# Token stages: the second product and all that follows it one pipeline step later, at the head of each engine's order

## The reference

```python
    x = x + _L0_conv_ref(_ln_c(x), ...)
    t = _to_tokens(x)
    t = t + _L0_ffn_ref(_ln_t(t), W1, b1, W2, b2)
    x = _from_tokens(t, x)
    x = x + _L1_conv_ref(_ln_c(x), ...)
    t = _to_tokens(x)
    t = t + _L1_ffn_ref(_ln_t(t), W1, b1, W2, b2)
...
        h = jax.nn.relu(_qlinear(x, W1, b1))
        y = _qlinear(h, W2, b2)
```

## Time and profile before

| | us |
|---|---|
| median of three runs | 2622.84 |
| lowest, highest | 2618.95, 2629.99 |
| the profiled execution, its own time | 2624.89 |
| its span | 2623.1 |
| TensorE, busy time in the span | 2272.7 (87%) |
| VectorE, ScalarE, GpSimd, busy | 1523.5, 1123.3, 450.0 |

### The profile page before, as it was taken

The page is one execution under the profiler, slowest core; times in us unless marked ns, Lnnn a source line. Parts: engine busy times, 40 slices in busy tenths (PEclk is TensorE's granted clock), DMA queues, the critical chain, the costliest instruction groups (busy, mean ns, idle before and its releaser), DMA issues. The chain is left out here.

```text
span 2623.1 us, 62156 instructions
## 1 busy us (share of the span) xinstructions
PE 2272.7 (87%) x21290; PEld 1247.5 (48%) x21290; DVE 1523.5 (58%) x2653; ACT 1123.3 (43%) x2338; POOL 450.0 (17%) x707
## 2 busy tenths in 40 slices
PE   6679778898996999999699999999976998688886
PEld 3344436667773333333266666666641232233332
DVE  3345401111113777777488888888842455577776
ACT  4346421111112888888532222222211111577776
POOL 7510015100100000000054444444410000000000
PEclk9789869999997999999899999999987999899999
DMA  6999989788874777877576666666628999333332
GB/s 154 260 254 270 253 284 303 230 263 262 285 245 91 142 142 146 152 142 145 100 155 144 142 142 142 142 143 143 144 86 162 240 267 237 87 102 106 105 102 78
DMA packets 533239, 458.55 MB, mean 175 GB/s; under 512 B 316476, under 2 KB 445444, under 8 KB 529778
## 3 DMA queue, kind: packets, MB, share of 16 engines
q1 hardware_dynamic: 462882, 425.87, 63.4%
q0 software_dynamic: 5744, 23.34, 3.7%
q10 hardware_dynamic: 64512, 7.88, 2.3%
HBM read 272.33 MB, written 186.40 MB: 175 GB/s over the span
## 5 line engine op out<-in xcount | busy, mean ns | idle before, releaser
L604 PE MATMUL gate_ps<-gate_data,gate_wt 64*64 64x289 f32 x6144 | 397.1, 416 | 39.2 <-issue 27.2
L604 PEld LDWEIGHTS gate_ps<-gate_data,gate_wt 64*64 64x64 f32 x6144 | 303.1, 136 | 134.3 <-issue 59.8
L662 DVE TENSOR_TENSOR gate_out<-gate_gelu,gate_ps 128x578 f32<-128x578 f32 x96 | 72.2, 756 | 399.3 <-PE gate_ps L604 343.7
L949 ACT CAST mix_h<-mix_bank 96x512 f16<-96x512 f32 x512 | 267.6, 593 | 7.1 <-PE mix_bank L900 3.2
L639 ACT ACTIVATE gate_gelu<-gate_ps 128x578 f32<-128x578 f32 x96 | 62.7, 653 | 367.8 <-PE gate_ps L604 331.2
L2036 PE MATMUL fus_bank<-fus_xt,fus_taps 76*32 76x512 f32 x1344 | 159.6, 626 | 28.4 <-DMA fus_shift<-gate_shift 23.5
L1031 DVE TENSOR_SCALAR mix_hb<-mix_h,mix_b1q 96x1024 f16<-96x1024 f16 x256 | 122.7, 479 | 93.6 <-ACT mix_h L949 93.6
L900 PE MATMUL mix_bank<-mix_xq,mix_w1q 112*96 112x512 fp8e5 x512 | 143.5, 382 | 29.1 <-ACT mix_h L949 23.0
L1039 DVE CAST mix_hq<-mix_hb 96x2048 fp8e5<-96x2048 f16 x128 | 156.5, 1223 | 19.5 <-DVE mix_hb L1031 16.9
L292 DVE COPY exp_out<-exp_y 128x384 f32<-128x384 f32 x192 | 102.1, 567 | 103.5 <-PE exp_y L255 52.1
L912 PE MATMUL mix_x_bank<-mix_hq,mix_w2q 96*112 96x512 fp8e5 x512 | 136.1, 388 | 29.9 <-DVE mix_hq L1039 27.7
(11 more groups left out here) (226 smaller groups left out, 4050.6 us busy)
## 6 DMA issues: line engine op xcount, KB each, us to landing
y<-exp_out SPq DMA_DIRECT2D x64, 816.0 KB, 12.2
gate_data<-y SPq DMA_DIRECT2D x24, 2176.0 KB, 17.6
g<-gate_out SPq DMA_DIRECT2D x48, 578.0 KB, 4.9
mix_sc<-g SPq DMA_DIRECT2D x31, 816.0 KB
gate_wt<-wm SPq DMA_DIRECT2D x96, 256.0 KB, 8.5
wav_strips<-xp SPq DMA_DIRECT2D x96, 204.0 KB, 3.8
wav_halves<-xp SPq DMA_DIRECT2D x48, 340.0 KB
init<-wav_init SPq DMA_DIRECT2D x48, 268.0 KB, 2.4
```

What stands on the lines that cost most here:

```text
L604: mm = pe.matmul(banks(a, v)[64 * g:64 * (g + 1), r], wt[q][64 * r:64 * (r + 1), 2 * a + g, n, :], src, start=n == 0, stop=n == 3)
L949: act.copy(h16[at.pair][:, m, h, :], bank[(2 * m + h) % len(bank)][0:HID, :]).then_inc(h16_ready, 1)
```

## The change

In both stages, `show`, `round_shown` and `add_shown` move from stage 3 to stage 4 and to the head of the lists of PE, ACT and DVE. What follows them (`centre_out`, `variance("out")`, `square("out")`, `root("out")`, `normalise`, both stores) also goes one stage later, in its old place of the list. On DVE `add_shown` now stands ahead of `add_residual`, on PE `show` stands ahead of `project`. `quantize_hidden` gets a wait: `hq` has two buffers, and the second product of step n-2 must be done with the one that step n writes. `LEAD` of the second stage goes from 4 to 8. No instruction that computes is added or removed.

```diff
-        LEAD = 12 if wide else 4
+        LEAD = 12 if wide else 8
...
-                staged(sp, 2 * N, SLOTS, [(0, load), (4, store_x2)] + [(7, store_norm)] * wide, LEAD)
+                staged(sp, 2 * N, SLOTS, [(0, load), (5, store_x2)] + [(8, store_norm)] * wide, LEAD)
...
-                pieces = [(0, project), (3, show), (2, hide(0)), (2, hide(1)), (1, variance("in")), (0, centre_in)]
+                pieces = [(4, show), (0, project), (2, hide(0)), (2, hide(1)), (1, variance("in")), (0, centre_in)]
                 if norm_dst is not None:
-                    pieces = [(0, project), (3, show), (2, hide(0)), (4, centre_out), (2, hide(1)), (1, variance("in")), (5, variance("out")), (0, centre_in)]
+                    pieces = [(4, show), (0, project), (2, hide(0)), (5, centre_out), (2, hide(1)), (1, variance("in")), (6, variance("out")), (0, centre_in)]
...
-                pieces = [(3, round_shown), (2, round_hidden(0)), (2, round_hidden(1)), (1, root("in")),
+                pieces = [(4, round_shown), (2, round_hidden(0)), (2, round_hidden(1)), (1, root("in")),
                           (0, square("in"))]
                 if norm_dst is not None:
-                    pieces = [(3, round_shown), (2, round_hidden(0)), (4, square("out")), (2, round_hidden(1)), (1, root("in")), (5, root("out")), (0, square("in"))]
+                    pieces = [(4, round_shown), (2, round_hidden(0)), (5, square("out")), (2, round_hidden(1)), (1, root("in")), (6, root("out")), (0, square("in"))]
...
                 def quantize_hidden(at):
                     dve.wait_ge(hb_ready, at.n + 1)
+                    if not isinstance(at.n, int) or at.n >= 2:
+                        dve.wait_ge(mixed, at.n - 1)
...
-                pieces = [(0, add_residual), (3, add_shown), (2, bias_hidden), (2, quantize_hidden), (1, quantize_norm)]
+                pieces = [(4, add_shown), (0, add_residual), (2, bias_hidden), (2, quantize_hidden), (1, quantize_norm)]
                 if norm_dst is not None:
-                    pieces.append((5, normalise))
+                    pieces.append((6, normalise))
```

## The result

The changed kernel takes 2649.78 us (median of 20 runs), the kernel before 2622.82 (median of 20). The ratio is 1.0091, with a 95% interval of 1.0065 to 1.0117: slower, by 27 us of the medians. The ratio leaves out two slow executions of the changed kernel (7396.48 and 2684.37 us); the median of the others is 2648.5. The forecast was 2634 with a range of 2605 to 2660.

The account below looks back on a forecast made before the run. The prediction took loops of waits to bound the stages, 6.94 us a step (first, PE) and 5.64 (second). +26 in the first, -12.6 in the second and -1.5 at its end give +11.7 on 2622.84: 2634 us, range 2605 to 2660.

Parts of the forecast that it names:

- the 5.64 loop: Second stage before the change: show, y16, hidden copies, hq and back to show, 5.64 us a step.
- The tie through x1's four slots: Both stages: x1 waits for the x2 just before it, a new one-step loop of 7.37 us (first), 5.43 (second).
- The wait for the logarithm at show: First stage: show at the head must wait for logarithm out, which project covered before; 0.25 us a step.
- Loop (b): First stage, PE and ACT alone: variance in to show, show, project, hide(0), hide(1); 7.25 us a step.
- the own wait: On DVE, x1 waits for the semaphore of the x2 just before it; taken as 0.04 us, at most 0.22.
- my own case: The forecast itself: 2634 us, own range 2615 to 2650, first stage at 7.2 to 7.5, second 5.3 to 5.5; chance 0.58.
- The -1.5 at the end of the second stage: Second stage's end: hide no longer stands behind a show waiting for hq; -1.5 us, between 0 and -3.
- The first (only the second stage feels it): Rival: first stage stays at PE's own 6.94 a step, the second gains; 2609 us, chance 0.12.
- The second (upper bounds of the two gaps): Rival: x2 to x1 and yb to x2 gaps on DVE both cost 0.22; 2667 us, chance 0.14.
- The third, that the own wait is free: Rival: DVE's waits on its own semaphore cost nothing, saving 0.33 in both tie loops; 2608 us, chance 0.07.
- The fourth: Rival: the change moves nothing, gains and losses fall on slack; 2623 us, chance 0.09.
- loop (a): First stage: show, y16, yb, x2, x1, variance in, both logarithms and back to show; 7.37 us a step.

Follow-up runs that it names:

- order-only kernel with a later store: Kernel before, second stage reordered at stage 3 (show behind hide, y16 behind hidden copies, add_shown last), x2 store one stage later, eight iterations written out: ratio 0.9897.
- The control: Kernel before with eight x1 buffers and loops unrolled by eight, nothing else changed: ratio 0.999, second stage at 5.64 a step.
- order-only run: Kernel before, second stage reordered at stage 3: show behind hide, y16 behind the hidden copies, add_shown last, four buffers, store unmoved: ratio 1.0175.

## Why the prediction was right, point by point

**The present loops.** The second stage's is confirmed: with the show taken out of its place the 5.64 loop disappears, and the order-only kernel with a later store cuts it another way. That PE holds the first stage at 6.94 was read from the rows and not tested; no kernel tried had a mean pitch below 6.96 there.

**The tie through x1's four slots.** This is shown, by both of its halves. Eight buffers take away the semaphore's part, the residual first takes away the order's part, and the second stage goes from 5.58 over 5.33 to 5.15. The control excludes the buffers as such.

**The wait for the logarithm at show.** This is shown too. Without the tie, putting project back ahead of show took the first stage from 7.33 to 6.98. The 0.25 read from the end of the first stage before is the 0.25 measured in its middle (1014.74 to 1014.99). Loop (b) is the next longest of the first stage: 7.25 forecast, 7.33 measured.

**The sizes.** The forecast had +0.43 a step in the first stage and -0.21 in the second; the pitches give +0.54 and -0.06. Two terms were too small, and both stand in both loops. `x2` to `x1` was taken as 0.73 and measured 0.79 to 0.83, 0.81 on average. The choice of 0.04 for the own wait, because "its other operands and counts are ready while the 0.69 run", was the step that failed; 0.10 to 0.14 is between my bounds, near the average gap of `yb` to `x2`, which was the nearer row. And variance to logarithm in the first stage, or variance to centre in the second, was taken from products that had not waited: 1.06 and 0.86, where behind a wait they are 1.15 and 0.94. The earlier trace rows had shown the longer record, 1.11, for a product behind a wait. Together these are 0.17 and 0.16 a step, where the pitches missed the sums of 7.37 and 5.43 by 0.14 and 0.15. That is some 8 to 9 us in each stage; the ends of the second stage (below) gave 2 us more than forecast, and in all the forecast was 15 us short.

**How right it was.** The direction, the two loops and the sign of each stage came out as forecast; the size did not. I had forecast 11 us more and measured 27. The two errors had the same sign, and the forecast was a difference of two larger terms, 26 and 14 us, so both counted in full. The 2650 us lie at the very edge of the range I gave for my own case (2615 to 2650), and both pitches lie just outside theirs (7.51 for 7.2 to 7.5, 5.58 for 5.3 to 5.5). That the time still lies inside the range of 2605 to 2660 owes something to its width. Of the three outcomes, "within 0.5%" had the highest chance (0.46); the one that came, slower by more, had 0.40.

**The ends.** The -1.5 at the end of the second stage was too small, and a cost at its beginning was taken as 0 and is not. The last three pitches are 3.41, 4.27 and 3.65, together 5.8 us less than the last three before, and the stage ends 0.9 sooner behind its last show; but the first show comes 3.1 later behind the first project (20.29 instead of 17.24). Together the ends gave 3.6 of the 7.2 us, and the pitch the rest.

**The rivals.** The first (only the second stage feels it) fell with the first stage's 7.51. The second (upper bounds of the two gaps) was half right: the `x2` to `x1` gap came out at 0.10 to 0.14 instead of 0.22, and the `yb` to `x2` gap at 0.21 to 0.24 in every other step of the first stage and 0.15 to 0.18 in the second, with 0.04 in the steps between. The third, that the own wait is free, is refuted by the run with eight buffers: the same two instructions are 0.61 apart without the wait and 0.80 to 0.83 with it. The Trainium skill, "VectorE: DVE Perf Modes", section "The DRAIN you can't avoid", speaks of a semaphore that is set after each copy. What costs here is the wait for it, and the page says nothing of that; that waits too are free was the prediction's own reading of it. No run here sets or leaves out a semaphore alone. The fourth fell with the 1.0091.

Costs taken as nothing: in the second stage the run with the first stage old shows none for stores, loads and the added wait. In the first stage, loop (a) with the measured terms (show to `y16` 1.08, `yb` 0.61, `x2` 0.48 on average, `x1` 0.81, its two parts 1.14, then 0.05, 1.15, 1.26, 0.67 and 0.25) is 7.50 against a pitch of 7.51, which leaves no room for them. That the loads keep their distance was right for this change, and the order-only run shows how it goes wrong when `x2` moves.

## What to carry to other kernels

Moving a piece to a later stage lengthens the life of what it reads: count the buffers, since the last free one turns a cross-iteration slack into a tie inside the iteration, and write the new one-step loop down before you gain from cutting the old one. Before a piece goes to the head of an engine's list, ask which wait the piece that stood there was covering. When a result moves on a compute engine, follow it to the DMA queue too, because the loads can stand behind its store.

## What the runs showed of the hardware that was not expected

The first product of PE behind a wait for `x1` takes longer to the next product than the same product without a wait: 0.94 or 0.95 (2414.09 to 2415.03, 2454.80 to 2455.75) against 0.86, with a recorded duration of 1.11 against 1.02. ACT, which waits for its result, starts 1.14 to 1.15 after it instead of 1.06 or 1.07. The rows have one more difference: the weight load of the product that waited starts together with it (both at 1011.66 in the changed kernel), that of the product that did not wait starts 0.21 ahead of it (2402.88 and 2403.09 in the kernel before). Whether that makes the 0.09 was not tried.

When DVE waits for its own last write, the next instruction starts 0.04 to 0.24 after the write's recorded end, depending on the place: 0.10 to 0.14 ahead of `x1`, 0.18 ahead of `hq`, and 0.04 or 0.21 to 0.24 ahead of the first stage's `x2`. Without the wait it starts 0.08 ahead of that end (0.61 behind the `x2` of 0.69, with eight buffers). Ahead of `x2` the short and the long gap go by the place in the unrolled loop: one by one in the changed kernel, two by two in the kernel before. Why was not tried.
